# Layer 3's opening inside layer 2, layer 0's second residual at step 10, and layer 1's first normalised graph made in layer 0's last stage

## The reference

```
h = relu(layernorm(x)); x = x + layer0(h)   # 4 heads, q k v, scores clipped to +-10, masked softmax per
                                            # chunk of 128 keys, projection, + h, layernorm, gamma, beta
h = relu(layernorm(x)); x = x + layer1(h)   # 4 heads, additive scores, masked softmax over nodes, elu
h = relu(layernorm(x)); x = x + layer2(h)   # 8 heads, additive scores with a prior, then W_out
h = relu(layernorm(x)); x = x + layer3(h):
    h1, h2, h3 = h @ W1, h @ W2, h @ W3
    e = leaky_relu(h1 @ h2.T, 0.2); e = where(adj > 0, e, -1e12)
    out = relu(softmax(e) @ h3)
```

## Time and profile before

| | us |
|---|---|
| median of 3 runs | 2028.11 |
| lowest and highest | 2024.01, 2032.48 |
| the profiled execution | 2026.8 |
| its span, from the first to the last instruction | 2024.6 |
| layer 0's block | up to 666 |
| layers 1 and 2 | 666 to 1643 |
| layer 3 | 1643 to 2024.6 |

### The profile page before, as it was taken

One profiled execution on the slowest core, in us unless ns is written; L12 is line 12 of the kernel. 1 busy time (PEld: TensorE's weight loads), 2 busy tenths in 40 slices (PEclk: granted clock), 3 DMA queues, 4 the chain that ended last, 5 costly groups with the idle time before them and its releaser, 6 DMA issues. The chain is left out here.

```text
span 2024.6 us, 36872 instructions
## 1 busy us (share of the span) xinstructions
PE 1650.5 (82%) x13620; PEld 1056.3 (52%) x13620; DVE 1603.9 (79%) x2710; ACT 1339.6 (66%) x1751; POOL 126.2 (6%) x130
## 2 busy tenths in 40 slices
PE   3998988988986577999999777977797748999997
PEld 1444443434433356777777556755675534555554
DVE  4888988988987557888888889898888747666764
ACT  2766666666663576777776989888888814554553
POOL 1000010010000100000000000000000000000000
PEclk7999999999998688999999878888888869999999
DMA  8634634635622311111111112111211120000000
GB/s 232 160 102 122 141 92 115 147 89 127 141 71 68 119 43 39 47 43 42 50 46 43 54 64 74 65 64 55 74 65 64 63 89 1 11 22 10 10 11 21
DMA packets 74922, 146.49 MB, mean 72 GB/s; under 512 B 11937, under 2 KB 34722, under 8 KB 74754
## 3 DMA queue, kind: packets, MB, share of 16 engines
q1 hardware_dynamic: 74754, 144.23, 25.4%
HBM read 101.85 MB, written 8.78 MB: 55 GB/s over the span
## 5 line engine op out<-in xcount | busy, mean ns | idle before, releaser
L1097 ACT ACTIVATE g<-s_all,steep_d 128x1024 fp8e4<-128x1024 f32 x608 | 642.3, 1135 | 40.6 <-DMA s_all<-s_rows 20.6
L1032 PE MATMUL acc<-parts,g 128*128 128x102 bf16 (+1 forms) x6144 | 417.2, 229 | 24.7 <-DVE sums L1188 24.5
L1032 PEld LDWEIGHTS acc<-parts,g 128*128 128x128 fp8e4 x6144 | 401.5, 100 | 57.4 <-issue 40.5
L1014 PE MATMUL post<-parts,edge 128*128 128x396 bf16 (+1 forms) x1024 | 233.7, 384 | 88.4 <-DVE base L1196 88.4
L583 ACT ACTIVATE e<-s_ps 128x1024 f32<-128x1024 f32 x256 | 248.1, 1022 | 24.5 <-PE s_ps L439 22.3
L1181 DVE TENSOR_TENSOR g<-g,edge 128x1024 int32<-128x1024 int32 x192 | 228.1, 1220 | 34.1 <-ACT g L1097 34.1
L732 DVE SCALAR_TENSOR_TENSOR e<-e,bound 128x1024 f32<-128x1024 f32 x160 | 191.0, 1228 | 43.4 <-ACT e L583 43.3
L1014 PEld LDWEIGHTS post<-parts,edge 128*128 128x128 fp8e4 x1024 | 102.5, 102 | 195.9 <-issue 111.5
L435 PE MATMUL s_ps<-qs,ks 128*128 128x512 f32 x512 | 193.5, 487 | 6.6 <-DMA ks<-split 4.9
L451 PE MATMUL sum_ps<-e,pick 128*32 128x256 f32 x2048 | 142.2, 396 | 67.6 <-DVE e L732 57.4
L1879 ACT ACTIVATE z<-z,shift 128x1024 f32<-128x1024 f32 x64 | 73.6, 1149 | 161.0 <-DVE shift L1955 161.0
(11 more groups left out here) (158 smaller groups left out, 2146.7 us busy)
## 6 DMA issues: line engine op xcount, KB each, us to landing
s_all<-s_rows SPq DMA_DIRECT2D x96, 512.0 KB, 3.7
inv_all<-inv_rows SPq DMA_DIRECT2D x256, 128.0 KB, 2.9
qs<-split SPq DMA_DIRECT2D x128, 128.0 KB, 3.2
ks<-split SPq DMA_DIRECT2D x128, 128.0 KB, 2.8
x<-in_x SPq DMA_DIRECT2D x8, 512.0 KB, 6.8
inv_rows<-inv SPq DMA_DIRECT2D x32, 128.0 KB, 1.8
adj_in<-in_adj SPq DMA_DIRECT2D x8, 512.0 KB, 4.1
out_x<-x SPq DMA_DIRECT2D x8, 512.0 KB, 3.2
```

Of the source, the lines that this page charges most:

```text
L1014: ins = pe.matmul(self.post[:, it % 2, 0:H * 3 * W1].rearrange("p (h k c) -> p h k c", h=H, k=3), self.c.edge[:, jt, it * P:(it + 1) * P], ...
L1032: ins = pe.matmul(self.acc[:, bank, o:o + self.NS], self.g[:, h % RING, jt, it * P:(it + 1) * P], self.upper[par][:, jt, h, :, :].rearrang ...
L1097: act.activation(self.g[:, h % RING, jt, :], self.s_all[:, h % 2, :], ACT.Relu, bias=self.steep_d[par][:, jt, h:h + 1], scale=STEEP, satur ...
```

## The change

Three things, all of them a move of work to an earlier place.

1. `residual` of a graph's second half is on DVE at step 10 (was 12), `output` on PE at step 10 (was 11), and `low` for k on DVE at step 9 (was 10). The last stage of layer 0 now also reads the copy `late` of h (POOL makes it there too), and `u` of the very last half is this `late`, so that `c.h` and `c.h_t` are free.
2. In layer 0's last stage DVE takes the statistics of graph 0 for layer 1 (steps 4 and 5), POOL makes the power, ACT the normalised graph (step 8); in `tail` PE turns it and ACT copies it to `c.h_t`, ahead of `output`. The first PE work of layer 1's block is then `pe_open`.
3. A class `Opening` holds layer 3's weights, masks and the turned and projected graph 0 in memory that outlives the block; masks and these two tiles lie in the `arena`, which is also `parts[0]` of layers 1 and 2 and free in the last stage of layer 2. The loads of weights and of the first four adjacency tiles are in the last stage but one of layer 2, the other four and all the computing in the last one.

```
             def stage(b, par, first, more):
-                if more and not first:
+                if not first:
                     wait_apart(c, pool, nm.h_ready, nm.upto(b - 1))
                     pool.tensor_copy(late[:, :, :], c.h[:, 1 - par, 4:8, :]).then_inc(late_ready, 1)
...
+                elif not more:
+                    pool.wait_ge(nm.h_ready, nm.upto(B - 1))
+                    pool.wait_ge(opened, 3)
+                    pool.tensor_tensor(c.rstd[:, :], c.var_eps[:, :], c.mhalf[:, :], ALU.pow).then_inc(opened, 1)
+                    pool.wait_ge(opened, 4)
+                    pool.tensor_tensor(c.offset[:, :], c.minus_mean[:, :], c.rstd[:, :], ALU.mult).then_inc(opened, 1)
...
-                    if i == 11 and not first:
+                    if i == 10 and not first:
...
+                pe.wait_ge(opened, 6)
+                pe.wait_ge(u_ready, 2 * B + 1)
+                for t in range(T):
+                    ins = pe.transpose(aux[:, t * P:(t + 1) * P], c.h[:, 0, t, :], c.ident[:, :])
+                ins.then_inc(opened, 1)
+                pe.wait_ge(opened, 8)
...
+                    elif i == 8:
+                        act.wait_ge(late_ready, b)
+                        act.wait_ge(u_ready, 2 * b + 1)
+                        act.wait_ge(opened, 5)
+                        for t in range(T):
+                            ins = act.activation(c.h[:, 0, t, :], c.x[:, 0, t, :], ACT.Relu, bias=c.offset[:, t:t + 1],
+                                                 scale=c.rstd[:, t:t + 1])
+                        ins.then_inc(opened, 1)
 
...
+                act.wait_ge(opened, 7)
+                act.wait_ge(x_updated, 2 * B + 1)
+                act.activation(c.h_t[:, :], aux[:, :], ACT.Copy).then_inc(opened, 1)
...
-                        elif i == 12:
-                            residual(b - 1, 1 - par, 1, more)
+                        elif i == 10:
+                            residual(b - 1, 1 - par, 1, True)
...
-                        elif i == 10:
+                        elif i == 9:
                             low(n, k_hi, bk, k_split, q_lo_stacked)
...
+                    elif not more:
+                        if i == 4:
+                            dve.wait_ge(x_updated, 4)
+                            for t in range(T):
+                                ins = dve.bn_stats(c.stats[:, t, :], c.x[:, 0, t, :])
+                            ins.then_inc(opened, 1)
+                        elif i == 5:
...
+    def sp_adj(self, sp, adj_in, tiles):
+        for t in tiles:
+            if t >= 4:
+                sp.wait_ge(self.adj_used, t - 3)
+            sp.dma_start(adj_in[:, t % 4, :], self.w["adj"][t * P:(t + 1) * P, :]).then_inc(
+                self.adj_loaded[max(t // 2 - 1, 0)], 16)
...
+    def pe_turn(self, pe, aux):
+        pe.wait_ge(self.w12_ready, 1)
+        self.norm(aux).pe_turn(pe, 0, 0)
+
+    def pe_q(self, pe, aux):
+        nm = self.norm(aux)
+        pe.wait_ge(nm.h_t_ready, nm.upto(0))
+        project_rows(pe, aux, self.w12[:, :], self.ht).then_inc(self.q_projected, 1)
...
+    def dve_bias(self, dve, adj_in, tiles):
+        for t in tiles:
+            dve.wait_ge(self.adj_loaded[max(t // 2 - 1, 0)], 64 if t < 4 else 32)
+            dve.tensor_scalar(self.bias[:, t, :], adj_in[:, t % 4, :], 0, NEG, ALU.is_le, ALU.mult).then_inc(self.adj_used, 1)
...
+                    if a is two and isinstance(b, int) and b == B - 2:
+                        if h == 0:
+                            third.sp_weights(sp)
+                        elif h % 2 == 1:
+                            third.sp_adj(sp, adj_in3, (h // 2,))
+                    elif a is two and isinstance(b, int) and b == B - 1 and h >= 4:
+                        third.sp_adj(sp, adj_in3, (h,))
...
-                one.pe_turn(pe, 0, 0)
+                pe.sem_inc(one.nm.h_turned, 1)
...
+                    if a is two and isinstance(b, int) and b == B - 1:
+                        if h == 0:
+                            third.pe_w12(pe, aux)
+                        elif h == 2:
+                            third.pe_turn(pe, aux)
+                        elif h == 4:
+                            third.pe_q(pe, aux)
...
-                one.act_h(act, 0, 0)
-                one.act_h_t(act, 0, 0)
+                act.sem_inc(one.nm.h_ready, 1)
+                act.sem_inc(one.nm.h_t_ready, 1)
...
+                    if a is two and isinstance(b, int) and b == B - 1:
+                        if h == 3:
+                            third.act_w12(act, aux)
+                            third.norm(aux).act_h(act, 0, 0)
+                        elif h == 6:
+                            third.act_h_t(act, aux)
+                        elif h == 7:
+                            third.act_q(act, aux)
...
+                    if a is two and isinstance(b, int) and b == B - 1:
+                        if h == 0:
+                            third.dve_stats(dve, aux)
+                        elif h < 5:
+                            third.dve_bias(dve, adj_in3, (h - 1,))
+                        elif h > 5:
+                            third.dve_bias(dve, adj_in3, (2 * h - 8, 2 * h - 7))
...
-            for dst, name in ((w1_t, "w1_t"), (w2_t, "w2_t"), (w3, "w3")):
-                sp.dma_start(dst[:, :], w[name]).then_inc(loaded, 16)
-            for t in range(T):
-                if t >= 2:
-                    sp.wait_ge(adj_used, t - 1)
-                sp.dma_start(adj_in[:, t % 2, :], adj[t * P:(t + 1) * P, :]).then_inc(adj_loaded[t % 2], 16)
...
-            def prepare(n, par):
-                stats(n, par)
-                for t in range(T):
-                    dve.wait_ge(adj_loaded[t % 2], 16 * (t // 2 + 1))
-                    dve.tensor_scalar(bias[:, t, :], adj_in[:, t % 2, :], 0, NEG, ALU.is_le,
-                                      ALU.mult).then_inc(adj_used, 1)
-                dve.wait_ge(adj_used, T)
 
...
-            walk(dve, prepare, stage, tail)
+            walk(dve, lambda n, par: None, stage, tail)
```

134 lines of the change are left out of this document (99 added, 35 removed).

## The result

| | before | changed |
|---|---|---|
| median, us | 2027.5 (4 runs) | 1999.96 (4 runs) |
| lowest to highest, us | 2024.0 to 2032.5 | 1999.1 to 2004.2 |
| span of the profiled execution, us | 2024.6 | 1997.2 |

The ratio of the times is 0.9866 (95% interval 0.9841 to 0.9892): 27.6 us less, where 24 to 25 were forecast. The way there is not quite the forecast one. The table follows the marks of the prediction through both traces; each figure is how much earlier (-) the mark comes than in the kernel before, summed up from the start.

The account below looks back on a forecast made before the run. No single engine was taken to bound the program. The terms -8.3 + 2.2 - 2.8 + 5.1 - 20.4 = -24.2 us led from 2026.8 to 2002.6, stated as 2003, with a range of 1990 to 2015 meant to hold 8 in 10.

Parts of the forecast that it names:

- Border into layer 1, -8.3: From layer 0 to layer 1: graph 0's chain is taken out, adjacency loads still hold DVE's edges, weighed values start 8.3 us earlier.
- The bound of 6.5: Border into layer 1: gain of 6.5 us if PE comes into its code as late as DVE at the other border.
- Layer 0's last stage, +2.2: Layer 0's last stage: DVE's statistics and aggregates for layer 1 and POOL's copy of `late` cost 2.2 us (1.0 to 3.0).
- The residual, -0.4 a stage: Layer 0, residual moved to step 10: 0.4 us less in each of seven stages, -2.8 in all (-7.7 to +3.5).
- No rival on this part: Three on layer 0's residual: whole wait returned (1979, 0.10), DVE's new wait paid in full (2020, 0.09), slow steps (2039, 0.03).
- the first: Layer 0's residual: ACT's 26.1 us of waiting for POOL are on the path, -26 instead of -2.8, 1979; chance 0.10.
- Layer 2's last stage, +5.1: Layer 2's last stage: preparing layer 3's opening there costs 5.1 us (3 to 7).
- its three terms: Layer 2's last stage: PE let go later 1.8 us, PE's turn and projection 2.9, other mask tiles 0.4.
- Border into layer 3, -20.4: From layer 2's last update to layer 3's first mask: 5.0 us left of 25.4, so -20.4 (-21.4 to -18.3).
- The paragraph on the Trainium skill's rule: Border into layer 3: a taken branch outside the engine's window fetches first, so the mask comes at about 6.1 us, time 2004.
- the cases under 2018: Outcomes counted as faster: the forecast (0.62), the first rival (0.10), loads holding layer 2's heads (0.08), border less shortened (0.08).

## Why the prediction was right, and where it was not

- **Border into layer 1, -8.3.** The mechanism held: PE's chain is out, the loads hold the edges. In the changed kernel the term is -5.8 (28.96 to 23.15 us from layer 0's end to the weighed values), below the bounds of 6.5 to 11.1. Its six loads took 4.92 us to issue. In six other runs with the same opening they took 2.9 to 3.5; there, with the edges in their old place, the values start 20.7 to 21.4 us after layer 0's end: -7.6 to -8.3. So the term held there, and the longer issue of the loads fits what the changed kernel lacks. GpSimd's reduction, which allows only some 2 to 3 us more, was not seen. The bound of 6.5 does not follow from the 4.01 us that it names.
- **Layer 0's last stage, +2.2.** The residual's marks give +2.4 (a gain of 6.3 us ahead of it, 4.0 behind), inside its 1.0 to 3.0.
- **The residual, -0.4 a stage.** DVE's wait, ACT's missing one and PE's 3.8 us came as drawn. The size was too small: 0.7 to 0.9 a stage in the middle, and 8.6 us in the median instead of 2.8, also outside its -7.7. The prediction had counted on the full clock and put the gain at 0 if the clock fell at step 11. It fell (0.80 and 0.78), and the stages were shorter all the same, so that this part of the working failed. More telling is what the step left out. It costed steps 12 and 10 and found them nearly equal, which they are. It never asked for step 11, where the wait of the one and the wait of the other are both gone. No rival on this part came true. ACT's whole wait did go, as the first has it, but the -26 did not come with it; DVE's new wait, which was held against that rival, is what a step at 11 avoids.
- **Layer 2's last stage, +5.1.** It is +3.1 between the last two combines and 3.8 with what stands on DVE ahead of them. Which of its three terms was too high no run shows.
- **Border into layer 3, -20.4.** It is -17.4. Two errors. A mask at 5.0 us with 1.98 us of products ahead of it lets PE start at about 3.0: it starts at 3.95, nearly DVE's whole 4.01. And the scores' 1.98 us of the earlier trace rows was taken for the lower clock, but that row ran at the full one (its stretch, 1664.2 to 1668, shows a granted clock of 1.00, 2.4 GHz); at the lower one four products take 3.78. The paragraph on the Trainium skill's rule gave 6.1 us for the border, nearer to the 7.93 than the forecast's 5.0.
- **The body of layers 1 and 2, 0.** Unforecast: 3.4 us less between the first weighed values and the combine before the last (889.11 to 885.67). No part of the change owns it. From layer 2's first combine to the one before the last it took from 387.5 to 397.6 us in the twelve kernels run here, and the two ends of that range have the same code there (the residual at 11 with the two reductions, and without). In them VectorE's busy time is 348.2 and 348.6 us and ScalarE's 339.7 in both, but TensorE's is 299.1 and 307.5, at a mean granted clock of 0.89 and 0.85. So the length goes with TensorE's clock. Why the clock differs stays open.
- **The end.** Once the first mask is there, layer 3 keeps all but 0.8 us.

By the marks of the two traces, layer 0 gained 3.8 us more than said and the stretch of layers 1 and 2 up to the last update 5.6 more (-0.5 instead of +5.1, the unforecast part among them), while the first border gained 2.5 less, the last one 3.0 less, and layer 3 lost 0.8. So the total was near partly by luck: errors of 9.4 us one way and 6.3 the other cancel. Two small sums of the prediction are off as well: 2002.6 and 1.3 make 2003.9, not 2003, and the chances of the cases under 2018 add up to 0.88, not 0.90.

## What to carry to other kernels

When a step is moved along a schedule written by hand, try its neighbours on both sides and look at what stands *behind* it on its engine: a 2.5 us block ahead of a weighing and long clips starved TensorE for 4 us, and ahead of short clips for 0.8 (and 1.9 at the next long ones). On an engine that bounds a stage, as VectorE does here, time costs its full length in each stage. And where a program jumps over code that it does not run, look for the price of the jump (here 3.4 us on TensorE); moving the code may only move the price to where the jump then is.

## What the runs showed of the hardware

- The way over the untaken branch costs PE 3.4 us at the border into layer 3 (3.95 against 0.54). With layer 3 ahead of it, the program's end is 3.6 us longer (7.2 against 3.6).
- TensorE's four score products took 3.78 us behind the far border (3.9 in the run with 11 us of work ahead of it), 3.58 and 1.95 us in the two runs that entered layer 3 nearby, both after 1.79 us of idleness: there both levels of the clock occur.
- GpSimd's first reduction over the partitions in layer 1 starts 10.0 to 11.7 us after the instruction before it, and an extra one in layer 0 changes nothing of that (11.06).
- Two clips of VectorE took 2.76 us beside GpSimd's copy of `late`, and 2.35 without it. The copy itself took 1.3 to 1.6 us beside them, 0.61 beside the end of a reciprocal and a short clip.
- Identical code of layer 2 differed by up to 10 us between kernels whose edits lie elsewhere, and was longer where TensorE's mean granted clock was lower (397.6 us at 0.85, 387.5 at 0.89). A gain of a few us read at a late mark is therefore not yet a gain of the edit.
